# An attention and wave layer on one core: the order of TensorE's work priced by tiling, the first loads reordered, and SyncE's issue times corrected

## The reference

```python
h = layernorm(x)
Q, K, V = split(h @ w_qkv)                     # 16 heads of 16
Q, K = rope(Q), rope(K)
a = softmax(where(causal, Q @ K.T * 0.25, -1e9)) @ V
x = x + a @ w_proj + b_proj
h = layernorm(x)
out = x + sqrt((h @ cos(theta + theta_noise))**2 + (h @ sin(phi + phi_noise))**2)
```

## Time and profile before

| | before |
|---|---|
| median of three executions | 2235.67 us |
| the profiled execution | 2240.03 us |
| its span, first to last instruction | 2238.3 us |
| mean granted TensorE clock | 0.966 of full |
| TensorE matmuls busy | 2070.9 us, 93% |
| VectorE busy | 1601.9 us, 72% |
| ScalarE busy | 1296.1 us, 58% |
| GpSimd busy | 870.6 us, 39% |
| DMA packets | 119561, of them under 2 KB 82246, under 8 KB 119110 |

### The profile page before, as it was taken

The page is one execution under the profiler, slowest core; times in us unless marked ns, Lnnn a source line. Parts: engine busy times, 40 slices in busy tenths (PEclk is TensorE's granted clock), DMA queues, the critical chain, the costliest instruction groups (busy, mean ns, idle before and its releaser), DMA issues.

```text
span 2238.3 us, 37555 instructions
## 1 busy us (share of the span) xinstructions
PE 2070.9 (93%) x12864; PEld 869.9 (39%) x12864; DVE 1601.9 (72%) x2868; ACT 1296.1 (58%) x1620; POOL 870.6 (39%) x1250
## 2 busy tenths in 40 slices
PE   4999999989999999999999999999999999999883
PEld 3333333334433344334443344334444344333331
DVE  4787777877778778787677767687777777778611
ACT  1346656655566565666567555665656565566571
POOL 4622324352444325343534434335244434432331
PEclk9889999999999999999999999999999999999996
DMA  5420222132212223222222222122122211221211
GB/s 159 115 62 23 73 61 88 42 103 60 82 55 80 61 61 88 65 84 87 75 70 77 72 65 79 58 75 84 56 77 71 81 60 52 73 72 32 78 58 43
DMA packets 119561, 159.87 MB, mean 71 GB/s; under 512 B 30662, under 2 KB 82246, under 8 KB 119110
## 3 DMA queue, kind: packets, MB, share of 16 engines
q1 hardware_dynamic: 118928, 155.22, 23.7%
q10 hardware_dynamic: 444, 2.26, 0.3%
HBM read 88.97 MB, written 50.86 MB: 62 GB/s over the span
## 4 chain that ended last, share of the span: by engine, by line
PE 62%; DMA 7%; DVE 7%; issue 7%; POOL 7%; ACT 5%; SPq 4%; POOLq 0%; DVEq 0%
PE banks L761 16%; PE banks L745 15%; PE banks L724 15%; PE banks L685 5%; DVE chunk_max L943 4%; PE banks L694 3%; ACT probs L831 3%; DMA rot<-raw 3%; PE banks L675 2%; PE banks L722 2%; DMA inverse<-inverses 2%; SPq L508 2%; PE banks L708 2%; POOL crossed L478 1%; SPq L525 1%
## 5 line engine op out<-in xcount | busy, mean ns | idle before, releaser
L943 DVE TENSOR_REDUCE chunk_max<-banks 128x1 f32<-128x512 f32 (+3 forms) x2240 | 1399.8, 671 | 433.6 <-PE banks L724 418.9
L831 ACT ACTIVATE probs<-banks 128x1024 f32<-128x1024 f32 (+3 forms) x1280 | 1074.7, 899 | 567.5 <-PE banks L745 543.1
L724 PE MATMUL banks<-stack_k,stack_q 96*128 96x512 bf16 (+3 forms) x2560 | 833.7, 357 | 35.3 <-DVE chunk_max L943 27.6
L745 PE MATMUL banks<-stack_q,stack_k 99*128 99x512 bf16 (+3 forms) x2560 | 694.4, 353 | 15.9 <-ACT probs L831 7.0
L761 PE MATMUL banks<-probs,v_one 128*17 128x512 f32 (+3 forms) x5120 | 539.0, 537 | 21.4 <-POOL probs L1078 20.2
L724 PEld LDWEIGHTS banks<-stack_k,stack_q 96*128 96x128 bf16 x2560 | 249.3, 99 | 406.2 <-DVE chunk_max L943 183.5
L745 PEld LDWEIGHTS banks<-stack_q,stack_k 99*128 99x128 bf16 x2560 | 220.9, 99 | 280.7 <-ACT probs L831 127.5
L1078 POOL TENSOR_SCALAR_AFFINE_SELECT probs<-probs 128x512 f32<-128x512 f32 x256 | 166.3, 655 | 314.1 <-ACT probs L831 307.8
L761 PEld LDWEIGHTS banks<-probs,v_one 128*17 128x17 f32 x5120 | 117.7, 97 | 303.0 <-issue 224.2
L722 PE MATMUL banks<-diag_mask,ident_bf 128*128 128x128 bf16 x1024 | 204.9, 225 | 12.7 <-DVE chunk_max L943 9.1
L722 PEld LDWEIGHTS banks<-diag_mask,ident_bf 128*128 128x128 bf16 x1024 | 100.3, 99 | 148.2 <-DVE chunk_max L943 75.3
(11 more groups left out here) (88 smaller groups left out, 1134.3 us busy)
## 6 DMA issues: line engine op xcount, KB each, us to landing
split<-parts SPq DMA_DIRECT2D x64, 384.0 KB, 2.6
stack_q<-split SPq DMA_DIRECT2D x384, 64.0 KB, 2.2
stack_k<-split SPq DMA_DIRECT2D x384, 64.0 KB, 2.2
rot<-raw SPq DMA_DIRECT2D x256, 64.0 KB, 2.0
sums<-o_raw SPq DMA_DIRECT2D x64, 256.0 KB, 2.1
xin<-x SPq DMA_DIRECT2D x16, 512.0 KB, 4.0
heads_t<-sums SPq DMA_DIRECT2D x28, 256.0 KB
mid<-x SPq DMA_DIRECT2D x14, 512.0 KB, 4.1
```

The costliest lines, as they stand in the source:

```text
L724: mm = nc.tensor.matmul(bank[:, n * wide:(n + 1) * wide], stack_q[u % 2][0:SPLIT_ROWS, t, h + n, j * P:(j + 1) * P], stack_k[u % 2][0:SPLI ...
L745: mm = nc.tensor.matmul(scores_bank[h][:, w0:SPAN], stack_k[u % 2][0:ROWS, j // SUB, h, (j % SUB) * P:(j % SUB + 1) * P], stack_q[u % 2][0 ...
L831: nc.scalar.activation(probs[:, g % PROBS, 2 * pair:2 * pair + 2, w0:SPAN], scores_pair[pair][:, :, w0:SPAN], ACT.Exp).then_inc(s_exp, 1)
L943: nc.vector.tensor_reduce(to, bank[:, 0:count * wide].rearrange("p (h n) -> p h n", h=count), AX.X, ALU.max).then_inc(s_emptied["DVE"], 1)
```

## The change

Five things are changed. (1) In the plan, TensorE's change of kind is now that between `values` and everything else, at the same 0.1; and for `RUN` (2.0 us) after a change, `STICK` (0.02 units) is added to the due time of a job that would change again. Value products were in pairs of steps already (`VALUES` is 2 in both). (2) `SLACK` goes from 0.2 to 0.4; block 1's `stats` follows block 0's `apply`; the projections of unit 1 follow `rows` of unit 0; a span's `v` follows its `qk`; the turn of all units but the first is planned 1.0 us after the split instead of 0.17. (3) SyncE's durations in the plan become those of several issues each (a fetch 5.4 instead of 1.0, a swap 2.4 instead of 0.3, and so on), with shorter lags after them. (4) First loads: the weights come as the first group alone and, behind x block 1 and the value weights, the other three; the tables come as the first span's columns and then the rest; TensorE waits for each where it is first used. (5) Two of the four crosswise copies of the first span are issued by ScalarE's queue; the fetch names the same bytes with heads and positions merged into one dimension.

```diff
-SLACK = 0.2
+SLACK = 0.4
-COARSE = ("max", "turn", "scores")
+TILED = ("values",)
+STICK = 0.02
+RUN = 2.0
+TURN_LAG = 1.0
...
-            job(("xload", n), "SP", 0.1, at, [("xt", n - 2, 1)], 4.2)
-            job(("stats", n), "DVE", 2.1, at, [("xload", n), ("apply", n - 2), begun(at - SLACK)])
+            job(("xload", n), "SP", 0.45, at, [("xt", n - 2, 1)], (4.8, 8.0)[n] if n < 2 else 4.2)
+            job(("stats", n), "DVE", 2.1, at, [("xload", n), ("apply", n - 2), *([("apply", 0)] if n == 1 else []), begun(at - SLACK)])
...
-                job(("qk", u, c, k), "PE", 0.86, at - HOLD * k, [("out", ("xt", n, k)), before_qk, ("rope", *ago, 1), begun(at - SLACK)])
+                job(("qk", u, c, k), "PE", 0.86, at - HOLD * k, [("out", ("xt", n, k)), before_qk, ("rope", *ago, 1), begun(at - SLACK), ("rows", u - 1, c) if u == 1 else begun(at - SLACK)])
...
-            job(("rot", u, c), "SP", 0.3, at, [("out", ("qk", u, c, 1)), ("rope", *ago, 1)], 2.4)
+            job(("rot", u, c), "SP", 2.4 if i else 1.2, at, [("out", ("qk", u, c, 1)), ("rope", *ago, 1)], 1.8)
...
-                    job(("rope", u, c, n), "DVE", 0.68, at, after)
+                    job(("rope", u, c, n), "DVE", 0.8, at, after, 0.0 if n < ROPE_OPS - 1 else None)
...
-            job(("keep", u, c), "SP", 0.1, at, [("rope", u, c, ROPE_OPS - 1), ("fetch", *ago)], 2.4)
-            job(("fetch", u, c), "SP", 1.0, at, [("keep", u, c), ("scores", u - 2, NSTEP - 1, 1)], 4.0)
+            job(("keep", u, c), "SP", 0.45, at, [("rope", u, c, ROPE_OPS - 1), ("fetch", *ago)], 2.4)
+            job(("fetch", u, c), "SP", 5.4, at, [("keep", u, c), ("scores", u - 2, NSTEP - 1, 1)], 2.2)
...
-                job(("v", u, c, j), "PE", 0.43, at - HOLD * (j > 0), [("out", ("xt", n, 1)), ("v", u, c, j - 1), begun(at - SLACK)])
+                job(("v", u, c, j), "PE", 0.43, at - HOLD * (j > 0), [("out", ("xt", n, 1)), ("v", u, c, j - 1), ("qk", 2 * u, c, KT - 1), begun(at - SLACK)])
...
-            job(("split", u, c), "POOL", 1.3, at - 0.2, [("rowmax", u, c)])
+            job(("split", u, c), "POOL", 1.3, at - 0.2, [("rowmax", u, c)], TURN_LAG if u else None)
-            job(("rows", u, c), "SP", 0.3, at, [("out", ("turn", u, c))], 2.4)
+            job(("rows", u, c), "SP", 1.7, at, [("out", ("turn", u, c))], 1.8)
...
-            job(("inverse", n), "SP", 0.2, at, [("keepinv", n), ("add", prev), ("inverse", n - 1), *free], 2.5)
+            job(("inverse", n), "SP", 1.1, at, [("keepinv", n), ("add", prev), ("inverse", n - 1), *free], 4.5)
...
-            change = e == "PE" and exact == (name[0] in COARSE)
-            found.append((max(at, free[e]) + TURN_COST * change, jobs[name][2], name))
+            change = e == "PE" and exact == (name[0] not in TILED)
+            stick = STICK * change if free[e] - since < RUN else 0.0
+            found.append((max(at, free[e]) + TURN_COST * change, jobs[name][2] + stick, name))
...
         if e == "PE":
-            exact = name[0] not in COARSE
+            if exact != (name[0] in TILED):
+                since = start
+            exact = name[0] in TILED
...
-                            sp.dma_start(tile[u % 2][slot * HD:(slot + 1) * HD, c, :, :],
-                                         rows.rearrange("(d h) n -> d h n", h=HG)).then_inc(s_fetch[i % 2], 16)
+                            tile = stack[u % 2][slot * HD:(slot + 1) * HD, c, :, :]
+                            sp.dma_start(tile.rearrange("p h n -> p (h n)"), rows.rearrange("(d h) n -> d (h n)", h=HG)).then_inc(s_fetch[i % 2], 16)
...
-                sp.dma_start(wqk[:, :, :, :], w_qk.rearrange("g p k n -> p g k n")).then_inc(s_wqk, 16)
+                sp.dma_start(wqk[:, 0, :, :], w_qk[0]).then_inc(s_wqk[0], 16)
                 load_block(1)
                 sp.dma_start(wv[:, :, :], w_v.rearrange("(k p) n -> p k n", p=P)).then_inc(s_wv, 16)
+                sp.dma_start(wqk[:, 1:GROUPS, :, :], w_qk[1:GROUPS].rearrange("g p k n -> p g k n")).then_inc(s_wqk[1], 16)
...
-                pe.wait_ge(s_wqk, 16)
-                pe.wait_ge(s_wv, 16)
-                pe.wait_ge(s_ones, 32)
...
+                        if i == 0:
+                            ins.then_inc(s_emptied["ACT"], 1)
+                            emptied(act, item)
+                            for own, other in HALVES[2:4]:
+                                act.dma_start(rot[own:own + 32, 0, :], raw[other:other + 32, 0, :]).then_inc(s_rot[0], 16)
+                            return
...
-                act.dma_start(cos_t[:, :], cosines).then_inc(s_tables, 16)
-                act.dma_start(sin_t[:, :], sines).then_inc(s_tables, 16)
+                for n, columns in enumerate((slice(0, SPAN), slice(SPAN, SEQ))):
+                    act.dma_start(cos_t[:, columns], cosines[:, columns]).then_inc(s_tables[n], 16)
+                    act.dma_start(sin_t[:, columns], sines[:, columns]).then_inc(s_tables[n], 16)
```

## The result

| | before | after |
|---|---|---|
| median | 2236.64 us | 2155.60 us (2153.69 to 2162.13) |
| ratio, with 95% interval | | 0.9647 (0.9613 to 0.9682) |
| span | 2238.3 us | 2151.9 us |
| mean granted TensorE clock | 0.966 | 0.978 |

A forecast was written before the change was run, and what follows sets the result against it. TensorE's order and rate were taken to bound 2135 us between filling and emptying. Head 14.5, joins 3, turn lag 7 and new order 5 made 29.5 off 2240.03: 2210.5, 2206 at the median, stated as 2205; range 2174 to 2232.

The forecast's parts named there:

- True issue times of SP: SyncE's true durations in the plan: move the order in the middle, gain nothing directly; 0, bounds -5 and +5 us.
- Switches to the value products: TensorE's value runs: 0.21 us for a run's two switches; stickiness joins 15 to 30 of 320 pairs, 3 us gained.
- Rival 3: Value pairs join and starve the other engines, so the kernel gets slower: 2255 us from 65 joins; chance 0.08.
- The right price's effect: TensorE's choices in the plan: a candidate behind a switch stays eligible as before and the due time chooses.
- the new order as a whole: Projections, transposes and finishes filling in earlier in TensorE's middle: 5 us gained, bounds 20 lost and 25 gained.
- `TURN_LAG` at 7: Turn planned 0.83 us later, so it waits less for the split: 7 us gained, bounds 0 and 14.
- The head: Start of the kernel, up to the first scores: 14.5 us gained, low bound 8, high bound 20.
- (a): Head, block 0's normalising ahead of block 1's statistics: ends at 12.8 instead of 21.0 us, 8.2 earlier.
- (b): Head, block 0's transposes, copies and two products: raw ready at 18.8 instead of 27.5 us, 8.7 earlier.
- (d): Head, the rope's last six operations kept together: done at about 25.9 us, 12.6 earlier.
- (e): Head, store of the parts, then fetch: landed at 36 us; first maximum product about 16 us earlier.
- the low bound's case: Head gains only 8 us: block 1's work falls into the rope, SP's other swap precedes the fetch, products at half clock.

The follow-up runs named there:

- before_sp_times: The kernel before with only SyncE's true durations and lags put in its plan (13 lines): 2202.8 us.
- old_sp_times: The changed kernel with SyncE's durations and lags of before in the plan, all else kept: 2225.2 us.
- stats_first: The changed kernel with block 1's statistics again ahead of block 0's normalising: 2160.4 us.

## Why the prediction was wrong

**By its own sign.** I had written that I am wrong if the middle changes by over 25 us either way; from the first scores to the last value product it changed by 78. The first maximum product (46.0, forecast 34 to 40) and the first scores (61.1, forecast 49 to 56) missed too. The runs of values (318), the turn's wait for GpSimd (9.1) and the tail (49.4) came as forecast.

**What bounds the kernel: half right.** TensorE's rate and order decide in the middle, but "idle time of theirs costs only where it makes TensorE wait" was then tested on the wrong rows. The chain of work that ended last had 7% on DMA, 7% on GpSimd and 4% on SyncE's queue, and I read the busy shares instead.

**True issue times of SP: the step that failed.** I wrote that "in the middle TensorE waits only 0.6 us for a DMA", so the true times "gain nothing directly", 0 with bounds of 5. They were worth 35 us alone (before_sp_times) and 70 us last (old_sp_times). TensorE's own rows name only its last releaser: it waits for a maximum or a mask, and the DMA stood one engine further back, in front of VectorE or GpSimd. Both rows were in the trace: VectorE for the inverses, 18.2 us in the middle, and GpSimd for the swaps, 78.8. Each of these engines runs its list in order, so all that is behind a wait in the list shares it. Removing the two, with every list as it was, gave 29 and 37 us.

**Switches to the value products: the cost right, the joins not.** There are 318 runs of values against 317, so no more pairs joined than before; 0.21 us a run is still paid, and the term of 3 should have been about 0. Rival 3, joined pairs that starve the others, did not occur.

**The right price's effect: wrong.** "That stays" was the failed sentence, by the counts above: I looked at whether a change of kind could exclude a candidate, and missed that under the old price values and the other f32 products were one kind, so that after values an f32 product was free and a maximum cost 0.1. Undone together with the stickiness, it costs 23 and 71 us.

**`SLACK`, with "the new order as a whole" at 5:** 22 and 29 us when undone. Its bound, 25, was about right, its middle was not. **`TURN_LAG` at 7:** the waits for the split fell as forecast (45.2 to 9.1 us), but the lag itself made the kernel 10 us slower, within the reach of a nudge.

**The clock, left out.** I took the half-rate time as given. It fell by up to 30 us between the first scores and the last value product, as it also did in the runs that only took waits away (49 to 39 us, 54 to 32).

**The head: 14.5 forecast, 7.5 measured.** These are the rows after that answer to the earlier trace rows:

```profile
9.79 1.38 DVE L904 TENSOR_SCALAR xin<-xin,mv,rstd 128x256 f32<-128x256 f32 x4 [2.33 <-POOL rstd L1040]
...
15.90 0.60 ACT L819 ACTIVATE raw<-banks 128x512 f32<-128x512 f32 x1 [2.01 <-PE banks L704]
...
23.00 1.40 DVE L891 BATCH_NORM_STATS2 stats<-xin 128x6 f32<-128x256 f32 x4
...
24.92 0.69 DVE L486 TENSOR_TENSOR crossed<-rot,sin_t 128x512 f32<-128x512 f32 x1
...
28.02 0.69 DVE L498 TENSOR_TENSOR parts<-crossed,parts 128x512 bf16<-128x512 f32 x1
28.50 2.41 SPq L515 DMA_DIRECT2D rot<-raw  x4
...
30.95 0.58 SPq L522 DMA_DIRECT2D split<-parts  x1
...
33.85 2.66 SPq L533 DMA_DIRECT2D stack_q<-split  x6
...
37.26 3.80 DVE L904 TENSOR_SCALAR xin<-xin,mv,rstd 128x256 f32<-128x256 f32 x4 [3.46 <-POOL rstd L1040]
...
41.12 1.97 PE L665 MATMUL banks<-ident,xin 128*128 128x128 f32 x8 [4.78 <-DVE xin L904]
42.92 3.21 PE L704 MATMUL banks<-x_t,wqk 128*128 128x512 f32 x4
45.97 0.22 PE L734 MATMUL banks<-diag_mask,ident_bf 128*128 128x128 bf16 x1
```

Steps (a) and (b) gave more than forecast: normalised 9.8 us earlier instead of 8.2, raw copied 11.0 earlier instead of 8.7. Step (d) lost it: block 1's normalising (21.70 to 23.08) and block 2's statistics stood before the rope's second product, which began at 24.92, not 22.0, and the rope ended at 28.7 instead of 25.9. In (e) the store stood behind the swap of span 1 (28.50 to 30.95), the low bound's case. And one assumption failed, that a shorter head leaves a block's projections for later: the fetch's issues were over at 39.3, but TensorE had the transposes and projections of all four blocks ahead of the first maximum product, and block 3 was normalised only at 41.06. That chain, not block 0's, set 46.0; stats_first shows it, where block 0 came 9.2 us later and the first maximum product 1.3. From there to the first scores it took 15.1 us instead of 16.3.

**The fetch's rewritten shape** stayed at nothing: 12288 packets of 4 KB before; the page after counts 64.0 KB and 2.2 us to landing for each, as before.

## What to carry to other kernels

Where engines run fixed lists, ask of each wait for a DMA on any engine what is queued behind it, and follow TensorE's waits two engines back. The chain of work that ended last does this by itself. Its share of DMA, GpSimd and queues says where to look, not how much there is to win: 14 points of 2238 us would be 313 us, and the time fell by 81. Stalls of 18 and of 29 us on an engine that was only three quarters busy cost 19 and 43 us in the units where they lay, and GpSimd's 79 us cost 37. When a plan's constants are changed, nudge one that should not matter, at both ends of the comparison, before reading a cause into 10 or 15 us: here such nudges moved the time by 14, 17 and, once, 33 us.

## What the runs showed of the hardware

Going over from bf16 or f32 products of the full array to the four-strip value products and back costs 0.09 and 0.12 us at full clock, and a change of data type none. After, it is the same: from a bf16 product of 512 columns to a value wave it is 0.31 us in the median, to an f32 product 0.22. The Trainium skill's page "TensorEngine Tiling (Array Packing)", section "Key Properties", says that a change of tiling mode drains TensorE; the 0.09 and 0.12 us of this trace agree with it. The four normalising instructions of a block (L904) took 1.38 us at 9.79, 2.37 at 28.81 and 3.80 at 37.26; in the last two stretches GpSimd worked beside them, in the first it did not, and those at 21.70, without GpSimd, took 1.38 again. No run here took the cause apart, but a plan that gives this job 1.4 us is short by up to 2.4, and block 3's was one of them.
